# A two-layer graph kernel: another order in row 0, events of the first layer moved by a half or two, three tiles multiplied whole, the last two results placed by themselves

## What is computed

```python
# x: 6144 x 128, adj: 6144 x 6144, both float32
def L0(x):                                   # first layer
    x_norm = layernorm(x, g_in, b_in)
    gate = hard_gate(x_norm @ Wn + bn, u)    # one number per row of x
    view2 = (adj * gate[:, None] * gate[None, :]) @ x_norm
    f = sigmoid(concat([x_norm, view2]) @ Wg + bg)
    fused = f * (x_norm @ W1 + b1) + (1 - f) * (view2 @ W2 + b2)
    return layernorm(fused + x, g_out, b_out)
def L1(x):                                   # second layer, hyperbolic
    xt = logmap0(mobius(weight, x, bias))
    h = expmap0(adj @ xt)                    # then relu of logmap0, expmap0
    return h_after_relu
x = layernorm(x + L0(x))
x = layernorm(x + L1(x))
```

## Time and profile before

| | |
|---|---|
| median of 3 runs | 964.14 us (962.69 to 965.74) |
| profiled execution | 965.12 us |
| its span | 963.3 us |
| PE busy | 912.4 us (95%) |
| DVE busy | 789.6 us (82%) |
| ACT busy | 682.2 us (71%) |
| granted clock of PE, mean | 0.993 |

### The profile page before, as it was taken

The page is one execution under the profiler, slowest core; times in us unless marked ns, Lnnn a source line. Parts: engine busy times, 40 slices in busy tenths (PEclk is TensorE's granted clock), DMA queues, the critical chain, the costliest instruction groups (busy, mean ns, idle before and its releaser), DMA issues.

```text
span 963.3 us, 12546 instructions
## 1 busy us (share of the span) xinstructions
PE 912.4 (95%) x4032; PEld 718.1 (75%) x4032; DVE 789.6 (82%) x1781; ACT 682.2 (71%) x1214; POOL 234.5 (24%) x202
## 2 busy tenths in 40 slices
PE   4998998999999999999999999998999999999993
PEld 3555777777887877888888888886687878778772
DVE  4667888988898788978695875859999898989894
ACT  6775786868686666757565465666888989788972
POOL 2210211111111111111020010201100755486563
PEclk9999999999999999999999999999999999999997
DMA  7978697776868676868574674756899999999980
GB/s 247 385 277 308 235 407 279 291 308 259 324 244 335 233 303 251 316 222 306 195 286 175 219 269 171 261 216 219 312 358 374 401 382 420 369 402 396 395 316 33
DMA packets 51825, 281.72 MB, mean 292 GB/s; under 512 B 6528, under 2 KB 8496, under 8 KB 20656
## 3 DMA queue, kind: packets, MB, share of 16 engines
q1 hardware_dynamic: 46432, 271.48, 73.9%
q10 hardware_dynamic: 5328, 9.44, 2.7%
HBM read 271.44 MB, written 9.46 MB: 292 GB/s over the span
## 4 chain that ended last, share of the span: by engine, by line
PE 45%; DVE 30%; DMA 8%; ACT 7%; POOL 6%; issue 4%; SPq 0%; POOLq 0%; DVEq 0%; ACTq 0%
PE PS L1021 12%; PE PS L1023 12%; PE PS L1022 12%; DVE AL L758 8%; DVE XGL L758 6%; DMA A<-in_adjT_dram 4%; DVE XTL L758 3%; PE PS L1019 2%; DVE BS L707 2%; PE PS L1110 2%; PE PS L1106 2%; POOL r_rs L452 2%; ACT AH L562 1%; POOL p_inv L452 1%; POOL SINV L476 1%
## 5 line engine op out<-in xcount | busy, mean ns | idle before, releaser
L758 DVE TENSOR_TENSOR AL<-A,AH 128x1024 fp32r<-128x1024 f32 x247 | 294.8, 1220 | 43.0 <-ACT AH L562 42.1
L562 ACT ACTIVATE AH<-A 128x1024 fp32r<-128x1024 f32 x247 | 253.0, 1058 | 106.6 <-PE PS L1023 84.4
L1021 PE MATMUL PS<-AH,XGH 128*128 128x512 f32 x344 | 137.2, 399 | 5.9 <-DVE AL L758 5.9
L758 DVE TENSOR_TENSOR XGL<-A,XGH 128x1024 fp32r<-128x1024 f32 x113 | 132.7, 1219 | 6.7 <-ACT XGH L562 6.3
L1023 PE MATMUL PS<-AH,XGL 128*128 128x512 f32 x344 | 134.1, 390 | 0.0
L1022 PE MATMUL PS<-AL,XGH 128*128 128x512 f32 x344 | 134.0, 390 | 0.0
L562 ACT ACTIVATE XGH<-A 128x1024 fp32r<-128x1024 f32 x113 | 113.1, 1056 | 14.0 <-DMA A<-in_adjT_dram 13.9
L1021 PE MATMUL PS<-AH,XTH 128*128 128x512 f32 x290 | 114.6, 395 | 2.4 <-DVE AL L758 2.3
L758 DVE TENSOR_TENSOR XTL<-A,XTH 128x1024 fp32r<-128x1024 f32 x92 | 109.8, 1221 | 5.4 <-ACT XTH L562 5.1
L1023 PE MATMUL PS<-AH,XTL 128*128 128x512 f32 x290 | 113.0, 390 | 0.0
L1022 PE MATMUL PS<-AL,XTH 128*128 128x512 f32 x290 | 112.8, 389 | 0.0
(11 more groups left out here) (245 smaller groups left out, 1560.7 us busy)
## 6 DMA issues: line engine op xcount, KB each, us to landing
A<-in_adjT_dram SPq DMA_DIRECT2D x243, 1024.0 KB, 6.8
GB<-gate_scratch SPq DMA_DIRECT2D x12, 256.0 KB, 3.6
XNT<-xnt_scratch SPq DMA_DIRECT2D x12, 256.0 KB, 4.1
XR<-in_x_dram SPq DMA_DIRECT2D x12, 256.0 KB, 4.8
x_scratch<-X SPq DMA_DIRECT2D x12, 256.0 KB, 7.7
xnt_scratch<-XNT ACTq DMA_DIRECT2D x6, 256.0 KB, 7.0
xnt_scratch<-X1T ACTq DMA_DIRECT2D x6, 256.0 KB, 6.2
XR<-in_x_dram ACTq DMA_DIRECT2D x4, 256.0 KB, 8.3
```

The costliest lines, as they stand in the source:

```text
L562: a.activation(high(m), A[:, n % RING, h * HW:(h + 1) * HW], ACT.Copy).then_inc(S["hi"], 1)
L758: v.tensor_tensor(low(m), A[:, n % RING, h * HW:(h + 1) * HW], high(m).bitcast(F32), ALU.subtract).then_inc(S["lo"], 1)
L1021: p.matmul(acc, hi[:, st], high(m)[:, mv], start=start, stop=False)
```

## The change

Cut to its core; in the tables a line or two stand for the rest, since the orders below show what the numbers do.

```diff
-WHOLE_FIRST = {0: range(12)}
+WHOLE_FIRST = {0: range(12), 1: (11,), 2: (11,), 3: (11,)}
...
-             "nm1": (10, 9), "resid": (10, 9), "curv0": (14, 3), "affine": (11, 10), "stats2": (13, 10),
-             "curv1": (18, 13), "nm2": (14, 12), "curv2": (18, 13), "tc": (20, 15), "k": (20, 19), "beta": (22, 21),
+             "nm1": (11, 9), "resid": (13, 9), "curv0": (14, 4), "affine": (13, 11), "stats2": (13, 11),
+             "curv1": (17, 15), "nm2": (14, 13), "curv2": (17, 15), "tc": (20, 16), "k": (20, 19), "beta": (22, 21),
...
-PE_FIRST = {"l0": (2, 0), "tr": (14, 12), "mx": (21, 19)}
+PE_FIRST = {"l0": (3, 1), "tr": (14, 13), "mx": (21, 19)}
...
-                    out.setdefault(end + after, []).append((event, o))
+                    out.setdefault(end + after[o >= NCH - 2], []).append((event, o))
...
-            load_a(0)
+            for n in range(2):
+                load_a(n)
...
+            for n in range(2, 5):
+                load_a(n)
...
-            for n in range(1, NCH + 3):
+            for n in range(5, NCH + 3):
...
-                    pow_half("s2max", 1, sinv[:, BLK:], sr[:, BLK:], "s2inv")
-                    pow_half("s2max", 2, sinv[:, 0:BLK], sr[:, 0:BLK], "s2inv")
+                    pow_half("s2max", 1, sinv, sr, "s2inv")
...
             gumbel_ln(1)
+            act.wait_ge(S["const"], 1)
+            a.activation(JUNK[:, 0:1], NHALF[:, 0:1], ACT.Exp)
             load_x(3)
             transposed(0)
-            act.wait_ge(S["const"], 1)
-            a.activation(JUNK[:, 0:1], NHALF[:, 0:1], ACT.Exp)
...
+            stats_pre(2)
             dve.wait_ge(S["gumbel"], 1)
             gate_begin(0)
-            stats_pre(2)
             gate_end(0)
...
             for k in range(NCH):
+                if k + 1 < NCH:
+                    half(2 * k)
                 if k + 2 < NCH:
                     transposes(k + 2)
                 if k + 1 < NCH:
-                    half(2 * k)
+                    half(2 * k + 1)
                 if k + 2 < NCH:
                     rows_and_logits(k + 2)
-                if k + 1 < NCH:
-                    half(2 * k + 1)
```

22 lines of the change are left out of this document (11 added, 11 removed).

## The result

The kernel after takes 959.86 us (median of 9 executions, 959.19 to 962.14) against 963.97 for the kernel before (median of 9): a ratio of 0.9953, 95% interval 0.9940 to 0.9966. Run again later it had 961.21 (12 executions) and 0.9965 (0.9952 to 0.9978). So it is faster by 3.4 to 4.5 us; 10.1 were forecast. The direction held; the first median lies inside the range of 950.5 to 960.8, near its slow end, and the second 0.4 above it; the size of the gain did not hold.

The account below looks back on a forecast made before the run. PE, busy 95% of the span, was taken as the bound. Row 0 0.6, l0 4.3, row ends with whole tiles 3.3, second layer's start 1.1, tail 0.8: 10.1 us off 964.1 gives 954.0, range 950.5 to 960.8.

Parts of the forecast that it names:

- Row 0: First row: an earlier start and fewer stalls gain 0.6 us, between -0.5 and 2.8; a late fourth x was the risk.
- l0 of row 1: Row 1's start: PE's 2.36 us wait goes, 1.36 by the later l0, the rest by an earlier gate column.
- l0 of rows 2 to 7: Later row starts: waits of 0.71, 0.43 and 0.80 us go, each under 1.36; with row 1 together 4.3.
- the rival on the slower side: Rows 1 to 6: later l0 delays "tr" by 1.36 us each and tile loads too; 4.9 us slower, 969.0; chance 0.05.
- Whole tiles: Last tiles, rows 1 to 3: row 1 costs 0.6, 0.3 returns; rows 2, 3 gain 0.25 each, plus 0.2 or 0.3.
- Row ends: Earlier curv1, curv2 save 0.5 to 0.8 us in rows 2 and 3; rows 4 to 6 gain 1.4; with whole tiles 3.3.
- Second layer's start: DVE is the bound from 657; the gate one split later fills its idle time, gaining 1.1 us, between 0 and 2.
- rival 2: Row 0 or 1: PE's longer idling brings another slow-clock stretch costing 1.7 us, 955.7; inside the main case's 0.63.
- The tail: After PE's last product: earlier last statistics and one power of 8 columns gain 0.8 us, between 0 and 1.1.
- Rival (1): Late fourth x at the start, row ends bound by loads: gain only 5.2 us, time 958.9; chance 0.20.
- Rival (4): Waits move from row starts to row ends; only tail and part of row 1 remain, about 962; chance 0.08.
- The statement of being wrong: Wrong if PE's splits wait as long as before, or the second layer takes another time from 740 to 925.

Follow-up runs that it names:

- u_l0: Kernel after with gate, part, m2m, l0, tanh, fuse, stats1 and nm1 of rows 1 to 6 at the places of before; 959.27 us, ratio 0.9949.
- row0_alone: Kernel before with only row 0's part of the change (orders of PE, DVE and ACT, early loads of tiles 1 to 4); 964.20 us, ratio 0.9995.
- split_l0: Kernel after with the l0 chain of rows 1 to 6 at before's places and last tiles of rows 1 to 3 split again; 959.07 us, ratio 0.9945.
- u_early: Kernel after with all places of rows 1 to 6 as before, whole tiles kept; 963.23 us, ratio 0.9990.
- u_row0: Kernel after with the whole of row 0 as before (order of PE, DVE and ACT, and SP's loads); 959.24 us, ratio 0.9944.
- best3_row0: best3 with the order of PE, DVE and ACT in row 0 as before, paced loads kept; 954.13 us, ratio 0.9899.
- best2: best1 with row 0 as before (order of PE, DVE and ACT, and SP's loads); 956.91 us, ratio 0.9917.
- before_again: Kernel before, unchanged, run again for a second profile; 964.36 us, ratio 1.0002.
- after_again: Kernel after, unchanged, run again for a second profile; 961.21 us, ratio 0.9965.
- late_mix: Kernel after with a third set of places at the second layer's start: nm1, resid one half later, curv1, curv2 one half earlier; 959.07 replaced by 958.21 us, ratio 0.9934.
- best3: Kernel after with row 0's tile loads paced, last tiles of rows 1 to 3 split, and late_mix's places; 953.57 us, ratio 0.9886.
- best3_again: best3, unchanged, run again for a second profile; 954.13 us, ratio 0.9885.
- u_whole: Kernel after with the last tiles of rows 1 to 3 split again, only row 0 whole; 958.53 us, ratio 0.9941.
- best1: Kernel after with last tiles of rows 1 to 3 split again and before's places at the second layer's start; 958.16 us, ratio 0.9936.
- paced: Kernel after with SP's load order as before and row 0's loads of tiles 2 to 10 each held until DVE read an x; 957.38 us, ratio 0.9925.
- u_late12: Kernel after with before's places for events at the second layer's start alone (c = 12 and 13); 959.07 us, ratio 0.9943.

## Why the prediction was right in sign and wrong in size

Three steps failed, and each is a term of the sum: which transfers the early tile loads hold up in row 0, the slack that PE was said to have at the end of row 2 (whole tiles), and whom DVE waits for where the second layer begins. By the ledger they make 1.9, 1.3 and 3.0 us, which is all of the 6.1 us by which the gain fell short. A fourth term, "l0", was counted for the wrong part of the change.

**Row 0 (forecast 0.6 gain, measured 1.3 loss).** The step that failed is the one on the loads: the prediction looked at the load of x whose issue was to move (the fourth) and let the early tile loads touch only that. Its issue did not move (8.09 against 8.31), so the third gated chunk's start after 28 was not the sign of a late fourth x that it was said to be. What the tile loads held up was the first store of the normalised rows and the fifth x. In all eleven profiles with tiles 1 to 4 issued early ACT waits 2.3 to 4.5 us for that store, and the second gated chunk starts at 23.4 as a mean, against 21.6 in the nine others, where it does not wait for it. In the same eleven DVE waits 3.6 to 6.5 us for the fifth x; in the nine others it does not wait there at all. The last gated chunk starts at 72.5 as a mean of the four profiles with before's row 0 and at 74.1 as that of the eleven, and PE's row 1 starts 8.8 us behind it in all. The circle of ACT and DVE was read rightly: 5.1 us apart wherever x is there.

**l0 of row 1 (2.4 forecast; 1.9 measured, or 2.5 with the same clock, by another cause).** The wait did go. But in u_l0 and row0_alone it goes with "l0" at its old place too, in split_l0 and u_early all but 0.26 and 0.51 of it; and with before's row 0 the later "l0" still waits 1.98 (u_row0) and 2.78 (best3_row0), though not in best2. So what removes most of it is the change to row 0: the gate column written earlier, and PE's own later start. The prediction had the gate column as the second half of the term; the 1.36 that it gave to the later "l0" are not seen in full in any run.

**l0 of rows 2 to 7.** Row 7: 0.80 forecast, 0.94 measured in every kernel with the new places. Rows 3 and 4 (1.14 forecast): nothing that shows, since the waits go without the later "l0" in u_l0, and row 3's 0.71 is missing from before_again too. The forecast counted a wait's whole length for one edit though other parts of the change, or chance, also removed it. "tr" waits 0.71 and 0.77 in rows 1 and 2 of after (0.48 and 0.56 before), 0.70 and 1.16 in after_again (0.48 and 0.71), so the rival on the slower side had its mechanism at a sixth to a third of its size per row.

**Whole tiles.** The step "in rows 2 and 3 PE is not the bound there" holds for row 3 alone. In rows 1 and 2 the tile costs its full 0.7 each, and the lead that it leaves DVE is worth nothing that shows at the next row's start. Forecast: 0.3 lost in row 1, 0.5 or more gained in row 2; measured: 1.5 lost.

**Row ends (forecast 2.4 in rows 3 to 6, measured 2.7 by u_early).** Mechanism and size were right: "curv1" and "curv2" earlier and "scale" later. Row 2's wait fell from 1.95 to 1.25, the 0.7 forecast as 0.5 to 0.8.

**Second layer's start (1.1 gain forecast, 1.9 loss measured).** The prediction named DVE as the bound from 657 on and then looked only at what the change takes off it, not at whom DVE waits for in the new places. The orders of the tables show it without a run: "stats1" at 8 with "nm1" still at 9, "curv2" at 15 with "tc" at 16, one split of 1.15 us between them, and between them a power on POOL. late_mix shows that both statements hold: 1.3 gained if the powers have their time (1.2 to 1.3 in the three kernels best3, best3_again and best3_row0), 1.9 lost if not.

**The clock (rival 2).** It did not come in after. In both its profiles the granted clock has one slow stretch in row 1, 3.4 us long, as in before's first profile; no second one in row 0 and none of twice the length. Granted clock of 78 to 88 in before, then of 78 to 88 and 88 to 98 in after, of 78 to 88 in u_whole, which had no slow stretch, and of both in row0_alone, which had one of twice the length (columns as in the earlier trace rows):

```profile
78.00:88.00 10.00, 6.74 (x20) 4.45 (x18) 6.28 (x8) 8.80 (x10) 0.00 (x0) 0.83 0.79 274
```

```profile
78.00:88.00 10.00, 6.41 (x20) 4.84 (x20) 9.85 (x12) 8.61 (x9) 0.00 (x0) 0.83 0.90 312
88.00:98.00 10.00, 10.00 (x47) 7.52 (x46) 7.91 (x12) 3.58 (x5) 0.00 (x0) 1.00 1.01 415
```

```profile
78.00:88.00 10.00, 6.41 (x26) 4.51 (x25) 9.79 (x14) 9.35 (x10) 0.00 (x0) 1.00 0.92 324
```

```profile
78.00:88.00 10.00, 6.41 (x16) 4.28 (x15) 8.84 (x14) 8.59 (x9) 0.00 (x0) 0.69 0.88 325
88.00:98.00 10.00, 10.00 (x46) 7.51 (x45) 8.16 (x9) 3.16 (x4) 0.00 (x0) 0.97 0.99 385
```

PE had waited 2.35 us ahead of row 1 in before and 3.59 in the other three. Halves 24 to 30 take 4.1 less than before's first without a slow stretch (u_whole), 2.5 with one (after), 1.4 with one of twice the length (best1): 1.2 to 1.6 us for each 3.4 us at the low clock, near the 1.7 of the rival. The long stretch came in row0_alone, late_mix and best1, none in u_whole and paced, and a stretch of 3.4 in row 0 in five of the fifteen profiles with the new order there (best3, best1, late_mix, split_l0, u_late12). So what the rival feared exists, behind the same wait in some executions and not in others, and may be part of the spread of the medians.

**The tail (0.8 forecast, 0.8 measured)** is right in each step. What was not forecast is the 0.8 at the last tile (halves 474 to 476), a wait for its load. It is 0.97 and 0.78 in before, 0.47 in after_again, and absent in after, but also in row0_alone, so it need not be the new places'; why is left open, and so are the losses of single executions between halves 342 and 474, up to 3.8 us in late_mix.

**The other rivals.** Rival (1) named 958.9, near the 959.9 of the first run, but that is luck: the start was late through the fifth x and the store and not through the fourth x, no wait at "l0" came back with it, and the row ends of rows 3 to 6 kept their gain instead of losing 2.0. Rival (4), waits that only change place, does not hold for rows 3 to 6 either; but PE does lose at the first split of row 1 (3.59 against 2.35) and at the second layer's start what it gained elsewhere.

**The statement of being wrong.** It said that the second layer would take another time from 740 to 925 only if the reading was wrong. It did in the first profile and not in the second, so that test had no value without a second profile. The other half was that PE's splits wait as long as before. They do, with 14.6 and 16.6 us against 15.4 and 13.2, and that sign was right: the waits gone at the ends of rows 3 to 6 are made up by the longer one ahead of row 1 and by those in the second layer.
